# The last mixture of experts of two batches by pages of one expert, in a four-layer fp32 stack on one Trainium2 core

## The reference, cut to what matters

```python
shared = silu(x @ sg_w.T) * (x @ su_w.T) @ sd_w.T                  # inner width 128
scores = sigmoid(x @ gate_w.T) + gate_bias                         # 64 experts
group_scores = scores.reshape(T, 8, 8).max(-1)                     # the best 4 of 8 groups stay
masked_scores = scores * mask
topk_w, topk_i = top_k(masked_scores, 6)                           # 6 experts a token
topk_w = topk_w / (topk_w.sum(-1) + 1e-8)
h = silu(x @ eg_w[e].T) * (x @ eu_w[e].T)                          # inner width 64
out = shared + sum over the six of topk_w * (h @ ed_w[e].T)
```

## Time and profile before

| | us |
|---|---|
| three runs | 1866.37, 1861.17, 1857.43; median 1861.17 |
| the profiled execution | 1862.18, of it span 1860.4 |
| PE busy | 1671.0 |
| DVE busy | 1175.6 |
| ACT busy | 771.9 |
| POOL busy | 750.9 |

### The profile page before, as it was taken

The page is one execution under the profiler, slowest core; times in us unless marked ns, Lnnn a source line. Parts: engine busy times, 40 slices in busy tenths (PEclk is TensorE's granted clock), DMA queues, the critical chain, the costliest instruction groups (busy, mean ns, idle before and its releaser), DMA issues. The chain is left out here.

```text
span 1860.4 us, 30824 instructions
## 1 busy us (share of the span) xinstructions
PE 1671.0 (90%) x10277; PEld 1113.9 (60%) x10277; DVE 1175.6 (63%) x3054; ACT 771.9 (41%) x1957; POOL 750.9 (40%) x976
## 2 busy tenths in 40 slices
PE   5755699899999899999999979699999999999999
PEld 4545377657756477565676654457756565656656
DVE  6857568867666477564775653757656555554655
ACT  2321254346537466273662643146627322232321
POOL 2441744347666287471874750026646100000000
PEclk7866799999999999999999988899999999999999
DMA  9010122100000000000000000000000564634352
GB/s 334 19 29 1 40 88 77 32 10 9 1 1 2 2 11 1 1 2 1 10 4 1 2 1 0 1 1 1 2 1 24 168 192 127 194 105 127 112 173 85
DMA packets 63964, 92.51 MB, mean 50 GB/s; under 512 B 11192, under 2 KB 29240, under 8 KB 63040
## 3 DMA queue, kind: packets, MB, share of 16 engines
q1 hardware_dynamic: 61760, 86.34, 15.1%
q0 software_dynamic: 2048, 4.20, 0.8%
HBM read 80.55 MB, written 9.96 MB: 49 GB/s over the span
## 5 line engine op out<-in xcount | busy, mean ns | idle before, releaser
L1617 POOL TENSOR_TENSOR rows<-rows,rinv 128x512 f32<-128x512 f32 x192 | 198.5, 1061 | 117.4 <-DVE rinv L1857 117.4
L2528 ACT ACTIVATE region_b<-psum 128x512 f32<-128x512 f32 x132 | 78.8, 597 | 259.4 <-PE psum L2490 259.4
L1781 ACT ACTIVATE rows<-psum,nmax 128x512 f32<-128x512 f32 x192 | 129.9, 682 | 123.5 <-DVE nmax L1850 123.4
L2502 PEld LDWEIGHTS psum<-region_c,region_b 128*128 128x128 f32 x1024 | 132.1, 192 | 56.8 <-issue 43.9
L2566 DVE TENSOR_TENSOR region_b<-region_b,psum 128x512 f32<-128x512 f32 x128 | 87.8, 686 | 123.7 <-ACT region_b L2528 121.3
L1849 DVE TENSOR_REDUCE lg<-psum 128x2 f32<-128x1024 f32 x128 | 155.7, 1216 | 3.3
L1966 POOL TENSOR_TENSOR rows<-rows,rinv 128x128 f32<-128x128 f32 (+2 forms) x192 | 127.1, 684 | 75.6 <-DVE rinv L2135 75.6
L2130 DVE TENSOR_REDUCE nmax<-psum 128x1 f32<-128x128 f32 (+3 forms) x256 | 113.7, 486 | 40.8 <-PE psum L2012 39.8
L1861 DVE COPY turned<-psum 128x512 f32<-128x512 f32 x128 | 88.2, 689 | 80.5 <-PE psum L1677 79.5
L1665 PE MATMUL psum<-region_a,region_b 64*128 64x256 f32 x1024 | 130.6, 392 | 5.9 <-ACT rows L1781 2.9
L2502 PE MATMUL psum<-region_c,region_b 128*128 128x128 f32 x1024 | 133.7, 276 | 1.7 <-DVE region_b L2574 1.7
(11 more groups left out here) (747 smaller groups left out, 3619.7 us busy)
## 6 DMA issues: line engine op xcount, KB each, us to landing
pt<-gates SPq DMA_DIRECT2D x128, 128.0 KB, 3.2
ysb<-gates SPq DMA_DIRECT2D x128, 128.0 KB, 3.5
region_a<-in_eg SPq DMA_DIRECT2D x32, 256.0 KB, 3.5
region_a<-in_eu SPq DMA_DIRECT2D x32, 256.0 KB, 3.6
region_c<-in_weights SPq DMA_DIRECT2D x32, 256.0 KB, 4.8
sorted<-kctx SPq DMA_DIRECT2D x2, 1536.0 KB, 14.6
region_b<-sorted SPq DMA_DIRECT2D x12, 256.0 KB, 3.5
made<-rows SPq DMA_DIRECT2D x12, 256.0 KB, 2.4
```

Source lines behind the costliest of these rows:

```text
L1617: nc.gpsimd.tensor_tensor(row(u, j), row(u, j), rinv[:, 2 * u + j:2 * u + j + 1].broadcast_to([P, S]), ALU.mult).then_inc(s.pn, 1)
L1781: nc.scalar.activation(row(u, j), s_bank(u, j), ACT.Exp, bias=nmax[:, 2 * u + j:2 * u + j + 1], accum_out=sum_column(u // T, u % T, j)).th ...
L2502: mm = nc.tensor.matmul(bank(7)[:, P * t:P * (t + 1)], htb[:, i % 2, P * t:P * (t + 1)], wd, start=(i == 0 and t == 0), stop=(i == n_items ...
```

## The change

Batches 1 and 2 leave the dense form. Batch 0 stays dense and moves ahead of attention_2(3), in a block that also routes batches 1 and 2; the pages are worked beside `back` of batch 3; batch 3 stays dense and last, and its block also gathers and adds the routed rows.

- `attention_2(1)` also issues six HBM-to-HBM copies that give the two new tables finite rows (7.4 MB and 64 KB).
- `backs` also loads the eight gate chunks of moe_3 and, behind its 33 steps, normalises batch 0 (`norm_ahead` at 33, 35).
- `moe_3_beside_route`: dense moe_3 of batch 0; beside it `route_3` normalises 1024 rows, makes the scores, picks six experts, ranks the picks (triangular product plus running sums), makes 48 columns of slots, 112 page owners (28 quads, the worst case, whatever the data), the shares, and the shared expert of both batches. POOL issues 48 scatters of 128 rows. SP waits for all of them at the end of the block.
- `attention_2f(3)` loads three quads of rows, then all eight gate and eight up chunks.
- `pages_3_beside_back`: 28 quads; `back(3)` is laid in at every third page, its 33 steps over pages 0 to 96, then the norm of batch 3.
- `moe_3_last`: dense moe_3 of batch 3 with the weights already there; POOL issues 48 gathers, DVE adds 24 products a batch at steps 14 to 19 and 27 to 32.

Before there were four moe_3 blocks, now there are three. The core of the diff:

```diff
+GROUP_3 = (1, 2)
+GT3, K6 = 2 * T, 6
+QUADS_3 = (K6 * GT3 + E3) // 4
+PAGES_3 = 4 * QUADS_3
...
+            def gpsimd(pool):                                  # route_3
...
+                pool.wait_ge(s.slots, 1)
+                for j in range(GT3):
+                    for k in range(K6):
+                        nc.gpsimd.indirect_dma_start(sorted_3[:, :], bass.IndirectOffsetOnAxis(ap=slots_3[:, j, k:k + 1], axis=0),
+                                                     xn_3[:, j, :], None).then_inc(scattered_3, 16)
...
+        def pages_3(s, s_late):
...
+            TURN_LAG, DOWN_LAG = 2, 3
...
+            def sync(sp):
+                for q in range(QUADS_3):
+                    if q >= 3:
+                        sp.wait_ge(s.xt, q - 2)
+                        load_pages_3(sp, s, q)
+                    n = q - DOWN_LAG - 1
+                    if n >= 0:
+                        store_rows(sp, n)
+                for n in range(QUADS_3 - DOWN_LAG - 1, QUADS_3):
+                    store_rows(sp, n)
+
+            def store_rows(sp, n):
+                lo = 4 * P * n
+                sp.wait_ge(s.yc, n + 1)
+                sp.dma_start(made_3[lo:lo + 4 * P, :].rearrange("(j p) d -> p j d", p=P), page_y3[:, n % 3, :, :]).then_inc(out_sem(n), 16)
...
+                for k in range(PAGES_3 + 4 * DOWN_LAG):        # tensor
+                    q, j = k // 4, k % 4
+                    if k == 0:
+                        turn_rows(0)
+                    if q < QUADS_3:
+                        up(q, j)
+                    if 0 <= q - TURN_LAG < QUADS_3:
+                        turn_hidden(q - TURN_LAG, j)
+                    if 0 <= q - DOWN_LAG:
+                        down(q - DOWN_LAG, j)
+                    if j == 2 and q + 1 < QUADS_3:
+                        turn_rows(q + 1)
+                    yield k
...
+                for k in range(PAGES_3 + 4 * DOWN_LAG):        # scalar
+                    q, j = k // 4, k % 4
+                    if k == 0:
+                        copy_rows(0)
+                    if j == 0 and 0 <= q - 1 < QUADS_3:
+                        silu(q - 1)
+                    if j == 0 and 0 <= q - 1 - TURN_LAG < QUADS_3:
+                        copy_hidden(q - 1 - TURN_LAG)
+                    if j == 2 and q + 1 < QUADS_3:
+                        copy_rows(q + 1)
+                    yield k
...
+                for k in range(PAGES_3 + 4 * DOWN_LAG + 1):    # vector
+                    q, j = k // 4, k % 4
+                    if j == 0 and 0 <= q - 1 < QUADS_3:
+                        used(q - 1)
+                        to_half(q - 1)
+                    if j == 0 and 0 <= q - 1 - DOWN_LAG:
+                        copy_sum(q - 1 - DOWN_LAG)
+                    yield k
...
-        moe_3_block(0, first=True)
-        moe_3_block(1)
-        moe_3_block(2, b_back=3)
-        moe_3_block(3)
+        pages_3_beside_back()
+        moe_3_last()
```

More of the change, by code:

```diff
@@ L350, in flamingo_kernel, with found_at_3 @@
+        hid_m, hid_t3 = part(region_b, 1024, [P, 2, 8, I3]), part(region_b, 2048, [P, 2, 4 * P])
+        def found_at_3(i, k, t):
+            n = (i * K6 + k) * T + t
+            return part(wide_2, D * n, [P, D]) if n < 32 else part(rows2, D * (n - 32), [P, D])
         hid = part(turned, 0, [P, HID, F1])
@@ L393, in flamingo_kernel, with fill_rows_3, copy @@
         made_1 = [nc.dram_tensor(f"made_1_{g}", (PAGES * P, D), FP32, kind="Internal").ap() for g in range(2)]
+        sorted_3 = nc.dram_tensor("sorted_3", (SPARE_3 + P, D), FP32, kind="Internal").ap()
+        made_3 = nc.dram_tensor("made_3", (SPARE_3 + P, D), FP32, kind="Internal").ap()
+        def fill_rows_3(sp):
+            def copy(dst, lo, rows):
+                sp.dma_start(dst[lo:lo + rows, :].rearrange("(p r) d -> p (r d)", p=P),
+                             sorted_1[0][0:rows, :].rearrange("(p r) d -> p (r d)", p=P)).then_inc(filled_3, 16)
+            for lo in range(0, SPARE_3 + P, PAGES * P):
+                copy(sorted_3, lo, min(PAGES * P, SPARE_3 + P - lo))
+            copy(made_3, SPARE_3, P)
         def load_inputs(sp, s, b, f):
@@ L1522, in keys_of, with attention_2 @@
             return copy
-        def attention_2(k, b, combined=None, last=None):
+        def attention_2(k, b, combined=None, last=None, also_load=None):
             s = sems(k % 2, ATTENTION_2)
@@ L2693, in moe_3_block, with moe_3_beside_route @@
-        def moe_3_block(b, b_back=None, first=False):
+            block_of(k, sync, sides[0], [*sides[1:], norm_ahead(s_ahead, xs[3], set_f, bank(6), keys_of(3), 4, 8, LN_EPS),
+                                         norm_ahead(s_first, xs[0], set_m, bank(7), copy_xnt, 33, 35)])
+        def moe_3_beside_route():
             k = next_block()
             s3 = sems(k % 2, MOE_3)
[L2696 to L2700, removed]
+            sr = sems(k % 2, ROUTE_3, s3)
@@ L2702, in first_loads @@
             def first_loads(sp):
                 for c in range(4):
-                    load_down_3(sp, s3, c)
+                    load_up_down_3(sp, s3, c)
             def sync(sp):
[L2707 to L2711, removed]
+                spread_gates_3(sp, s3, True)
@@ new lines, in sync, with pages_3_beside_back, first_loads @@
+                store(sp, s3, 0)
+                sp.wait_ge(scattered_3, 16 * K6 * GT3)
+            block_of(k, sync, moe_3(s3, 0, True), [route_3(sr, bank(5), bank(6))], first_loads)
+        def pages_3_beside_back():
+            k = next_block()
+            s1 = sems(k % 2, SPARSE_3)
+            s2 = sems(k % 2, BACK, s1)
+            s_late = sems(1 - k % 2, LATE_3, sems(1 - k % 2, MOE_3))
+            def first_loads(sp):
+                for c in range(CH3):
+                    load_down_3(sp, c, s1.down_in)
+            block_of(k, pages_3(s1, s_late).sync, pages_3(s1, s_late),
+                     [paced(back(s2, B - 1, bank(6), bank(7), set_f, back_1), lambda n: 3 * n),
+                      norm_ahead(s1, xs[B - 1], set_m, bank(6), copy_xnt, 3 * 33 + 1, 3 * 35)], first_loads)
@@ L2713, in flamingo_kernel, with moe_3_last, sync @@
+        def moe_3_last():
+            k = next_block()
+            s3 = sems(k % 2, MOE_3)
+            combined = combine_3(sems(k % 2, LATE_3, s3))
+            def sync(sp):
+                spread_gates_3(sp, s3, False)
+                combined.sync(sp)
+                store(sp, s3, B - 1)
+                sp.wait_ge(stored, 16 * B)
+            block_of(k, sync, moe_3(s3, B - 1, False), [combined])
         fronts_beside_setup()
```

439 lines of the change are left out of this document (401 added, 38 removed).

## The result

The changed kernel took 1886.2 us (median of 4 runs, 1881.5 to 1888.1), the kernel before 1860.6 beside it: a ratio of 1.0141, 95% interval 1.0122 to 1.0160, so slower by 1.4%. The forecast was 1878 us in a range of 1845 to 1917. The profiled span is 1879.7 us against 1860.4 before, 19.3 more; the sum of the forecast said 16.7.

A forecast was written before the change was run, and what follows sets the result against it. The four moe_3 blocks were taken as bound by PE work, the new pages by waiting for rows. Terms 4.7+109+212+97 = 422.7 us against 406.0, +16.7, gave 1878 us, range 1845 to 1917.

The forecast's parts named there:

- The mechanism: Pages: each load of rows waits behind a store needing the same step's `copy_sum`, exposing its round trip; 7.6 us a round.
- A: Rival for the pages: loads come in time, a quad costs 3.7 us, block 140 us, whole 1806 us; chance 0.15.
- C: Rival for the pages: PE stays at 1.2 GHz, 9.0 us a round, block 251 us, whole 1917 us; chance 0.11.
- B: Rival for the pages: loads land in 2.7 us, round 6.7 to 6.8, block 194, whole 1855 or 1860 us; chance 0.14.
- The round: Pages, transposes through copies, silu, store and load to the next transposes: 7.5 us, 7.6 with the low clock; 23 rounds, 175 us.
- `back`'s intrusions: Pages: pieces of `back` ahead of silu and `used`, two exponentials at 3.3 us each and four smaller ones, together 10 us.
- The routing block: Dense batch 0 with the routing beside it: 109 us, between 105 and 119.
- The cover that I named: Routing block: POOL's scatters end at 99 us and land at 102, under the block's 109, so they cost nothing.
- The end of `backs`: The norm of batch 0 stands behind everything else in `backs`, uncovered: +4.7 us.
- The last block: Dense batch 3 with gathers and adds: 95.2 us plus 0 to 5, taken as 1.5 for the stores: 97 us.
- The sum: Norm, routing, pages and last block: 4.7+109+212+97 = 422.7 us against 406.0 before, +16.7.
- Rival D: POOL's transfers, 1.5 us apart, set the ends: scatters end at 113 us, gathers 2 us late; +6, 1884 us; chance 0.04.

The follow-up runs named there:

- the fresh quad off the ring: The changed kernel with DVE's `copy_sum` of quad q-4 moved ahead of `used` and `to_half` of quad q-1: pages block 182.5 us, whole 1956.3 us.
- both edits: The changed kernel with SP's store one quad later and DVE's `copy_sum` ahead of `used` and `to_half`: 1911.9 us, 1.0256 of the kernel before.

## Why the prediction was right, and where not

**The mechanism** was right and is shown: with the store one quad later, 71 us go from the pages; with the fresh quad off the ring, 34 to 35. Of the rivals, A is what the edit makes and not what the kernel does. C's low clock is there (0.80), and to raise it to 0.92 was worth under 5 us. B's landings of 2.7 us occur only as the least.

**The round** was put at 7.6 and takes 6.95 undisturbed. Of the 0.65 between them 0.3 is the landing: 3.2 us in the median of 28 loads, where I took 3.5 from the earlier trace rows. That median mixes loads issued close behind another (up to 7.9) with lone ones. The three lone ones behind a store there (298.21, 306.24 and 314.27) landed in 3.3, 3.2 and 4.9 us, so neighbours on the queue are at most part of the difference.

```profile
DMA to landing us min/median/max: 2.7/3.2/4.1
```

The Trainium skill, DMA: Bandwidth & Descriptors (Anatomy of one DMA), states its fit of 2.0 us plus the bytes at 436 GB/s for transfers that GpSimd issues. Put to this load, which SP issues, it gives an estimate of 2.6 us; the trace has 0.6 more.

Another 0.2 is overlap: silu starts 0.11 us before the row copy has ended, `copy_sum` 0.08 before `to_half` has. And the 0.1 that was added for the low clock does not show in undisturbed rounds.

**`back`'s intrusions** were put at 10 us. The 22 rounds between loads take 175.2 us and 22 times 6.95 is 152.9, so what is over is 22 us: 15 of the 22 rounds are longer than 7.25 us, and I had counted six pieces that would stand in the way. Counted as the forecast counts, from the transposes of quad 4 (1587.41) to those of quad 27 (1773.02), the 23 rounds take 185.6 us, 25.8 over 23 times 6.95. The two exponentials are as forecast: their rounds take 10.4 us each, 3.4 to 3.5 over, for 3.3. The other 19 us stand against 3.4 forecast for four smaller pieces. In the round from 1643.94 on, for one, `back` has 4.5 us of PE work, most of it between the row transposes and the products that silu waits for, and the round takes 10.0. Some of the excess can be the low clock of those rounds; with the pauses filled the 22 rounds behind the first are 5.6 us shorter.

This is the term that was mis-sized most, and that the sum came out is luck: the 23 rounds and `back` were put at 175+10 = 185 and took 185.6, since the round is 15 us too long in the forecast and `back` 16 us too short. The rest of the block: 6.2 us to the first product for 5, 12.2 to the transposes of quad 4 for 10.5, 12.4 behind those of quad 27 for 11.5. Together 216.4 for 212.

**The routing block** took 115.4 for 109. PE is busy for 105.9, 2 more than my sum (the first 31 us have a clock of 0.91), its pauses are 7.2 in place of 4.1, and from its last product to the next block it takes 2.25 us in place of 0.93. The slots came 47.6 us into the block and not 38, so the last scatter was issued at 110. The cover that I named was nearly gone, but the block without scatters took 114.6, so they were not yet its end.

**The end of `backs`** is as forecast: 4.9 us from the last add to the end of the norm, for 4.7.

```profile
1206.54 1.19 PE L690 MATMUL psum<-weights,xn 128*128 128x128 f32 x4 [3.92 <-DVE xn L680]
```

It does not show in the sum, since the rest of attention 2 and `backs` came out 5.9 shorter; why was not tried. The last block took 94.3 for 97: in the first measurement DVE never waited for a gather.

**The sum** was +16.7 and the trace has +19.3. Against the forecast the routing took 6.4 more, the pages 4.4 more and the last block 2.7 less; all other blocks together, the norm among them, came out 0.8 less than before, where 4.7 more were booked for the norm.

**What the forecast did not hold** is the 50 us a block that POOL's transfers cost in the later measurements. Rival D looked only at when they end, never at what they do to the others while they are issued; there the kernel takes 1996 us, far over the range of 1917, and the routing block 165, over the 119 that the forecast had named as a sign of wrong terms. That the first measurement fell inside the range is in this respect luck. The earlier trace rows could not show it: the gathers there stand 1.27 us apart, but only four in a row, and the longest row of indirect transfers in that kernel is twelve scatters (from 262.6 to 276.7).

A version that beats both kernels was not measured. The later store gives 145.0 us of pages; in the sum of the first measurement that would be about 1815 us, an estimate from 1886.2 less 71, since no experiment met the conditions of the first one. In those that were met, the best was 1911.9 with both edits, against 1863.4 for before.

## What to carry to other kernels

A transfer inherits the wait of whatever stands ahead of it on its queue: write out, for each load, what the store before it waits for, and in which step that happens. One more step of distance took a third off this stage, a shorter ring half as much, a higher clock 2% at most. And transfers that POOL issues by the dozen are to be looked at for what they do to the other engines, more than once and on more than one chip, before they are called hidden.

## Unexpected in the hardware

- The same kernel took 1886.2 us in one measurement and 1995.6 in another; the kernel before, without indirect transfers in those stages, took 1860.6 to 1866.7 in all of them. Three chips show the long form; since the chip of the short one is not known, it is open whether the chip or something else sets the two apart.
- While POOL issued 48 indirect transfers 1.25 us apart, ACT and DVE stood in the long form with all that they wait for done, ACT for 28.1 us at a stretch. With at most three in flight it stays; without SP's broadcasts it stays; without POOL's transfers it goes. The same 48 at the same distance did nothing of the kind in the first measurement, and what the engines stand for is open.
- In those blocks PE's granted clock is 0.80 to 0.84, where the short form has 0.98 and 1.00.
